# First stage of a fused two-layer block: scores of a head as one matmul of 48 stacked rows, filled by way of DRAM

## The chip, the cores and the metric

The kernel runs on one core of a Trainium2 chip. The core has a matrix engine (TensorE, PE in the profile; its weight loads are PEld), a vector engine (VectorE, DVE), a scalar engine (ScalarE, ACT), GpSimd (POOL) and a queue engine that only issues transfers (SyncE, SP). They run at the same time and wait for each other by semaphores. The metric is the device time of one execution in microseconds, the median of several runs.

## What is computed

The program is a block of two layers, each a gated attention with context tokens and a gated expert network. The change lies in the first attention. Cut to that:

```python
# x: 16 x 112 x 256, ctx: 16 x 375 x 256, 16 heads of 16
q = split_heads(layernorm(x) @ Wq.T + bq)          # 16 rows per head
k = split_heads(ctx @ Wk.T + bk)
v = split_heads(ctx @ Wv.T + bv)
scores = einsum('bhqd,bhkd->bhqk', q * 16**-0.5, k)
scores = scores + ((1 - mask) * -10000)[:, None]
attended = einsum('bhqk,bhkd->bhqd', softmax(scores), v)
x = x + tanh(g_xattn[0]) * merge_heads(attended)
# then: 2 of 8 linear experts per token; a second attention with 16 heads of 64; 2 of 8 two-layer experts
```

## The kernel before

Three stages follow one another: `phase_attention_small_heads` (first attention and the linear experts), `phase_attention_large_heads` (second attention and routing) and `phase_experts`. To keep float32 accuracy with float16 matmuls, each operand is split into a high part (HI) and the rest (LO), and a product is made of three: high by high, high by low, low by high (`PASSES`).

The first stage goes through 16 batches of 112 queries and 375 keys. Each engine runs its own program, written out by hand: `body(b, par)` for a batch, with sixteen slots `s`, one for each head. In slot `s` TensorE makes the scores of head `s` (`scores`, L593), transposes the probabilities of head `s - 2` (`transposes`, L602) and multiplies those of head `s - 4` with the values (`values`, L616). Between these it puts a piece of the projections of the next batch (`item`, L509: keys in slots 0 and 1, normalized x in 2, queries in 4, values in 5 to 7) and a piece of the experts of the batch before (`ditem`, slots 7 to 14). The order on TensorE is fixed. VectorE takes the scores from PSUM, adds the mask and finds the row maxima (`maxima`, L837), and makes the low part of the transposed probabilities (`plo`, L842). ACT makes the exponentials (L701) and the high part (`phi`, L708). There are two PSUM buffers for scores.

Scores of a head have 16 rows to contract. Before the change, one matmul contracts 128 rows. `k_stack` holds 64 rows of the keys' high part and below them 64 rows of their low part, for four heads at a time (a group `g`). The weights of the queries are doubled on the host, so that `q_f` (128 rows) has each group's 64 rows twice. `q_masked` holds for each head of a group these rows with those of the three other heads at zero; VectorE clears both of its buffers once at the start (L949). The first matmul takes the high part of the queries (against high and low keys), the second takes their low part. So a head needs two matmuls of 375 columns:

```python
for part in (HI, LO):
    last = pe.matmul(ps_s[h % 2][0:T, 0:C], q_masked[par][:, part, m, g * T:(g + 1) * T],
                     k_stack[par][:, g, :], start=(part == HI), stop=(part == LO))
```

`k_stack` and `q_masked` are filled from `k_s` and `q_s` by transfers between places in SBUF that SP issues: four for the keys (`stack_keys`, L344) and eight for the queries (`mask_queries`, L353) for each batch. SP's program for a batch is one list in a fixed order: mask, residual, tokens, context (`load_tokens`), keys, queries, a clearing of rows in DRAM for the third stage (`clear_rows`, L362, 1032 KB), store. The queries come from ACT (L665), which writes `q_f`, and GpSimd, which splits them (L431, L433). The transfers for batch `b + 1` are made during batch `b`; those for batch 0 stand ahead of the loop.

The second stage makes its scores (L1567) with 64 rows for each head, in pairs of heads on rows 0 to 63 and 64 to 127; all its other matmuls have over 64 rows. Its projections are at L1474, its values at L1582.

Of the kernel before, what the change touches and what calls it, by code (L numbers as in the profile page):

```python
# [112 lines left out]
def phase_attention_small_heads(nc, x, ctxT, mask, g_xattn, g_ffn, wq, wk, wv, bq, bk, bv, wg, we, be, consts,  # L113
                                x2_dram, next_w, next_w_dram, xs_dram):


    with ExitStack() as ctx:
# [8 lines left out]
        wqkv_f = sb("wqkv_f", [128, KT, 512 + 512 + E], F32)  # L126
        wqkv = sb("wqkv", [128, 2, KT, 512 + 512 + E], F16)
# [9 lines left out]
        wq_s = wqkv[:, :, :, 0:512].rearrange("p s k (g m) -> p s k g m", g=GROUPS)  # L137
        wk_s = wqkv[:, :, :, 512:768]
        wv_s = wqkv[:, :, :, 768:1024]
        wg_s = wqkv[:, :, :, 1024:1024 + E]  # L140
        bq_c = sb("bq_c", [128, GROUPS], F32)
# [18 lines left out]
        q_f = sb("q_f", [128, GROUPS * T], F32)  # L160
        q_s = sb("q_s", [128, 2, GROUPS * T], F16)
        q_masked = [sb(f"q_masked{i}", [128, 2, 4, GROUPS * T], F16) for i in range(2)]
        k_s = sb("k_s", [128, 2, 2, C], F16)
        k_stack = [sb(f"k_stack{i}", [128, GROUPS, C], F16) for i in range(2)]
# [60 lines left out]
        s_zq = sem("zq")  # L225
# [21 lines left out]
        s_qmask = sem("qmask")  # L247
        s_kstack = sem("kstack")
        s_score = sem("score")
# [29 lines left out]
        QMASK = 16 * 8  # L279
# [11 lines left out]
        WPARTS = ((512, 768), (0, 512), (768, 1024 + E))  # L291
# [13 lines left out]
        def _(sp):  # L305
            sp.dma_start(ctx_f[:, :, :], ctxT[0]).then_inc(s_cload, 16)
            sp.dma_start(wqkv_f[:, :, 512:768], wk).then_inc(s_wk, 16)
            sp.dma_start(x_in[:, :], x[0]).then_inc(s_xload, 16)
            sp.dma_start(wqkv_f[:, :, 0:512], wq).then_inc(s_wq, 16)
            sp.dma_start(wqkv_f[:, :, 768:1024], wv).then_inc(s_wv, 16)  # L310
            sp.dma_start(wqkv_f[:, :, 1024:1024 + E], wg).then_inc(s_wv, 16)
# [37 lines left out]

# [1984 lines left out]
```

## Time and profile before

| | |
|---|---|
| runs | 1442.60, 1450.26, 1454.12 us; median 1450.26 |
| profiled execution | 1443.42 us, of which the span from the first to the last instruction is 1441.8 us |
| mean granted TensorE clock | 0.944 of full speed |
| busy, share of the span | PE 88%, DVE 76%, ACT 70%, POOL 57% |
| DMA | 175.19 MB, mean 122 GB/s |

Busy time is the time in which an engine had at least one instruction under way. Matmuls overlap in the pipeline, so what one costs is the step from its start to the next one's start. The first stage ends at about 440 us, the second runs from about 500 to 1200 us, and the third takes the rest.

### The profile page before, as it was taken

To read this page: it belongs to the slowest core of one execution; us is meant where nothing else is said; L and a number is where in the kernel's file an instruction comes from. 1 tells how busy PE (TensorE), PEld (TensorE's weight loads), DVE (VectorE), ACT (ScalarE), POOL (GpSimd) and SP (SyncE) were. 2 spreads that over 40 slices of the span, in tenths; PEclk is the share of its full clock that TensorE was granted. 3 is DMA by queue.
4 is the path that set the end of the run, shared out by engine and by line. 5 is a ranking of instruction groups with operands and counts; after the bars stand their busy time and mean duration, and the time that the engine had idled before them with its cause. 6 is when DMAs were issued, how large, how long until landed. Compare 5 with 4: busy or idle time off the path is not lost. (4 is left out here: it accounts for less than half of the span.)

```text
span 1441.8 us, 44028 instructions
## 1 busy us (share of the span) xinstructions
PE 1264.8 (88%) x13508; PEld 916.7 (64%) x13508; DVE 1092.9 (76%) x3110; ACT 1003.9 (70%) x2584; POOL 827.7 (57%) x1204
## 2 busy tenths in 40 slices
PE   5999999999985599999998999999999985389994
PEld 3788888888864245656665556656566653278993
DVE  4899999999984268887887877878788873367772
ACT  3988788887883368787776777777787872155662
POOL 3645444454455445777676776777677675045663
PEclk9999999999997699999999999999999996599997
DMA  6233343333400148877666766767576784753323
GB/s 172 86 120 112 106 121 98 118 99 121 120 24 17 48 92 160 159 137 148 136 148 136 151 137 140 141 145 156 122 146 138 146 186 85 285 173 60 61 35 74
DMA packets 303968, 175.19 MB, mean 122 GB/s; under 512 B 250234, under 2 KB 291586, under 8 KB 300720
## 3 DMA queue, kind: packets, MB, share of 16 engines
q1 hardware_dynamic: 287632, 130.94, 40.8%
q0 software_dynamic: 13168, 35.80, 9.8%
q10 hardware_dynamic: 3024, 6.47, 1.6%
q8 instruction: 98, 1.61, 0.5%
q14 instruction: 46, 0.38, 0.1%
HBM read 64.48 MB, written 41.96 MB: 74 GB/s over the span
## 5 line engine op out<-in xcount | busy, mean ns | idle before, releaser
L1663 ACT ACTIVATE b_prob<-b_prob,b_top 112x487 f32<-112x487 f32 x256 | 178.9, 699 | 42.8 <-DVE b_top L1789 40.9
L1296 POOL TENSOR_TENSOR b_halves<-b_prob,b_halves 112x487 f16<-112x487 f32 x128 | 152.3, 1190 | 88.4 <-ACT b_halves L1688 86.6
L1474 PE MATMUL b_ps_p<-w_s,b_tok_s 128*128 128x512 f16 (+1 forms) x768 | 187.7, 381 | 5.6 <-DVE b_k_s L1776 5.3
L1474 PE MATMUL b_ps_p<-b_tok_s,w_s 128*128 128x487 f16 x768 | 188.0, 384 | 4.7 <-POOL b_tok_s L1290 3.7
L1789 DVE CUSTOM_DVE_ANT_0 b_prob<-b_ps_s,b_keep 112x487 f32<-112x487 f32 x256 | 167.7, 656 | 32.1 <-PE b_ps_s L1567 31.8
L701 ACT ACTIVATE a_prob<-a_prob,a_top 112x375 f32<-112x375 f32 x256 | 156.4, 611 | 4.5 <-DVE a_top L837 3.4
L1688 ACT ACTIVATE b_halves<-b_prob 112x487 f16<-112x487 f32 x256 | 156.0, 609 | 0.4
L837 DVE CUSTOM_DVE_ANT_0 a_prob<-a_ps_s,a_keep 112x375 f32<-112x375 f32 x256 | 138.6, 541 | 21.8 <-PE a_ps_s L593 19.2
L1582 PEld LDWEIGHTS b_ps_o<-b_v_s,b_pT 128*128 128x128 f16 (+1 forms) x3072 | 124.9, 100 | 32.7 <-DMA b_pT<-b_halves 11.0
L1582 PE MATMUL b_ps_o<-b_v_s,b_pT 128*128 128x64 f16 (+1 forms) x3072 | 136.1, 195 | 9.0 <-DMA b_pT<-b_halves 8.9
L842 DVE TENSOR_TENSOR a_pT<-a_ps_t,a_pT 125x336 f16<-125x336 f32 x256 | 128.6, 503 | 18.4 <-ACT a_pT L708 12.4
L602 PE MATMUL a_ps_t<-a_const,a_prob 112*125 112x112 f32 x768 | 127.8, 275 | 9.0 <-ACT a_prob L701 7.2
L602 PEld LDWEIGHTS a_ps_t<-a_const,a_prob 112*125 112x125 f32 x768 | 113.9, 189 | 31.3 <-ACT a_prob L701 22.5
L593 PE MATMUL a_ps_s<-a_k_stack,a_q_masked 128*112 128x375 f16 x512 | 126.5, 329 | 6.7 <-DMA a_q_masked<-a_q_s 6.1
L1474 PEld LDWEIGHTS b_ps_p<-b_tok_s,w_s 128*128 128x128 f16 x768 | 67.3, 100 | 96.4 <-issue 27.0
L1474 PEld LDWEIGHTS b_ps_p<-w_s,b_tok_s 128*128 128x128 f16 (+1 forms) x768 | 70.7, 105 | 85.1 <-DVE b_k_s L1776 14.1
L1776 DVE TENSOR_TENSOR b_k_s<-b_ps_p,b_k_s 128x487 f16<-128x487 f32 x128 | 84.5, 661 | 52.3 <-ACT b_k_s L1644 51.9
L1794 DVE TENSOR_TENSOR b_halves<-b_prob,b_halves 112x487 f16<-112x487 f32 x128 | 123.6, 965 | 0.0
L1567 PE MATMUL b_ps_s<-b_k_s,b_q_s 64*112 64x487 f16 x768 | 109.2, 391 | 14.8 <-issue 14.5
L708 ACT ACTIVATE a_pT<-a_ps_t 125x336 f16<-125x336 f32 x256 | 115.3, 450 | 9.8 <-PE a_ps_t L602 8.9
L1651 ACT ACTIVATE b_v_s<-b_ps_p 128x512 f16<-128x512 f32 (+1 forms) x128 | 76.2, 595 | 54.7 <-PE b_ps_p L1474 53.7
L1784 DVE TENSOR_TENSOR b_v_s<-b_ps_p,b_v_s 128x512 f16<-128x512 f32 (+1 forms) x128 | 87.9, 687 | 28.7 <-ACT b_v_s L1651 27.6
(262 smaller groups left out, 3063.0 us busy)
## 6 DMA issues: line engine op xcount, KB each, us to landing
xs<-a_blank SPq DMA_DIRECT2D x14, 1032.0 KB, 4.0
c_w_pool<-w_split SPq DMA_DIRECT2D x8, 1600.0 KB, 10.9
b_wch_f<-in_w_experts POOLq DMA_DIRECT2D x32, 384.0 KB, 4.9
w_split<-b_wch_s POOLq DMA_DIRECT2D x32, 384.0 KB, 4.0
a_ctx_f<-in_ctxT SPq DMA_DIRECT2D x16, 375.0 KB, 3.9
a_k_stack<-a_k_s SPq DMA_DIRECT2D x64, 93.8 KB, 2.8
b_ctx_t<-in_ctx SPq DMA_DIRECT2D x16, 375.0 KB
c_xt<-xs SPq DMA_DIRECT2D x35, 129.0 KB, 2.5
```

What stands on the lines that cost most here:

```text
L593: last = pe.matmul(ps_s[h % 2][0:T, 0:C], q_masked[par][:, part, m, g * T:(g + 1) * T], k_stack[par][:, g, :], start=(part == HI), stop=(p ...
L602: last = pe.transpose(ps_t[h % 2][0:KB0, j * T:(j + 1) * T], prob[:, h % RING, j * KB0:(j + 1) * KB0], ident[0:T, 0:T])
L701: act.activation(prob[:, h % RING, :], prob[:, h % RING, :], ACT.Exp, bias=top[:, h % RING:h % RING + 1], scale=-1.0, accum_out=sums[par][ ...
L837: dve.tensor_tensor_reduce(prob[:, h % RING, :], ps_s[h % 2][0:T, 0:C], keep[par][:, :], -SCALE0, 3e38, ALU.add, ALU.min, top[:, h % RING: ...
L842: dve.tensor_tensor(pT[0:KB0, h % RING, LO, :, 0:T], ps_t[h % 2][0:KB0, 0:NB0 * T].rearrange("p (j n) -> p j n", j=NB0), pT[0:KB0, h % RIN ...
L1296: pool.tensor_tensor(halves[:, h % TURN, LO, 0:NK], prob[:, h % RING, 0:NK], halves[:, h % TURN, HI, 0:NK], ALU.subtract).then_inc(s_lo[1], 1)
L1474: last = pe.matmul(out, sta(a, k), mov(m, k), start=(k == 0 and n == 0), stop=(k == tiles - 1 and n == 2))
L1582: last = pe.matmul(ps_o[h // 8][:, col:col + D1], pT[0:k, h % TURN, a, j, :], v_s[par][0:k, m, j, h * D1:(h + 1) * D1], start=(h % 8 == 0 ...
L1663: act.activation(prob[:, h % RING, 0:NK], prob[:, h % RING, 0:NK], ACT.Exp, bias=top[:, h % RING:h % RING + 1], scale=-1.0, accum_out=sums ...
L1688: act.activation(halves[:, h % TURN, HI, 0:NK], prob[:, h % RING, 0:NK], ACT.Copy).then_inc(s_hi, 1)
L1789: dve.tensor_tensor_reduce(prob[:, h % RING, 0:NK], ps_s[h % 3][0:T, 0:NK], keep[par][:, :], -SCALE1, 3e38, ALU.add, ALU.min, top[:, h % R ...
L1794: dve.tensor_tensor(halves[:, h % TURN, LO, 0:NK], prob[:, h % RING, 0:NK], halves[:, h % TURN, HI, 0:NK], ALU.subtract).then_inc(s_lo[0], 1)
```

## The change

A head's 16 rows of queries are stacked three times in 48 rows, as high, high, low, and its keys as high, low, high. One matmul over these 48 rows then makes all three products. Even heads lie in rows 0 to 47, odd heads in rows 64 to 111. The query weights are no longer doubled in SBUF: of each group only the first 64 columns are loaded, and the projection makes two blocks of 128 rows in place of four. Heads are spread over rows of `k_s` and `q_s`, so that the stacks are filled by way of two DRAM buffers, `keys` and `queries`: SP writes `k_s` or `q_s` out, waits until that has landed, and reads six pieces back (two halves, three parts).

```diff
+        q_stack = [sb(f"q_stack{i}", [128, H // 2, T], F16) for i in range(2)]
-        k_stack = [sb(f"k_stack{i}", [128, GROUPS, C], F16) for i in range(2)]
+        k_stack = [sb(f"k_stack{i}", [128, H // 2, C], F16) for i in range(2)]
...
+            def keys_out(c, par):
+                need_all(sp, settled, (s_ihi, 6, c, P_K + 2), (s_ifree, PI, c, P_K + 2), (s_kstack, NSTACK, c - 1, 0))
+                sp.dma_start(k_dram[par], k_s[:, :, :, :]).then_inc(s_kout, 16)
             def stack_keys(c, par):
-                need_all(sp, settled, (s_ihi, 6, c, P_K + 2), (s_ifree, PI, c, P_K + 2), (s_score, H, c - 1, 1))
+                need_all(sp, settled, (s_kout, 16, c, 16), (s_score, H, c - 1, 1))
+                rows = k_dram[par].rearrange("(r a d) s t c -> a s d r (t c)", a=2, d=D0)
                 for a in range(2):
-                    for part in (HI, LO):
-                        sp.dma_start(k_stack[par][64 * part:64 * part + 64, a::2, :],
-                                     k_s[64 * a:64 * a + 64, part, :, :]).then_inc(s_kstack, 16)
-            def mask_queries(c, par):
-                need_all(sp, settled, (s_qlo, 1, c, 1), (s_score, H, c - 1, 1))
-                for m in range(4):
-                    for row in (D0 * m, 64 + D0 * m):
-                        sp.dma_start(q_masked[par][row:row + D0, :, m, :], q_s[row:row + D0, :, :]).then_inc(s_qmask, 16)
+                    for i, part in enumerate(K_PARTS):
+                        sp.dma_start(k_stack[par][64 * a + D0 * i:64 * a + D0 * (i + 1), :, :].rearrange("d (r t) c -> d r (t c)", t=KT),
+                                     rows[a, part]).then_inc(s_kstack, 16)
+            # queries_out and stack_queries: the same with q_s, q_dram, q_stack, s_qout, s_qstack
...
             def body(b, par):
...
+                if ahead(b, 1):
+                    keys_out(b + 1, 1 - par)
                 if ahead(b, 2):
                     load_tokens(b + 2)
                 if ahead(b, 1):
                     stack_keys(b + 1, 1 - par)
-                    mask_queries(b + 1, 1 - par)
+                    queries_out(b + 1, 1 - par)
                 clear_rows(b)
+                if ahead(b, 1):
+                    stack_queries(b + 1, 1 - par)
...
-                    for g in range(GROUPS):
-                        last = product(ps[:, g * T:(g + 1) * T], lambda a, t: wq_s[:, a, t, g, :],
+                    for j in range(KT):
+                        last = product(ps[:, j * T:(j + 1) * T], lambda a, t: wq_s[:, a, t, j * 128:(j + 1) * 128],
                                        lambda a, t: xT[:, a, t, :])
...
-                for part in (HI, LO):
-                    last = pe.matmul(ps_s[h % 2][0:T, 0:C], q_masked[par][:, part, m, g * T:(g + 1) * T],
-                                     k_stack[par][:, g, :], start=(part == HI), stop=(part == LO))
-                last.then_inc(s_score, 1)
+                rows = slice(64 * (h % 2), 64 * (h % 2) + STACK)
+                pair = KT * (h % 8 // 2) + h // 8
+                pe.matmul(ps_s[h % 2][0:T, 0:C], q_stack[par][rows, pair, :], k_stack[par][rows, pair, :],
+                          start=True, stop=True).then_inc(s_score, 1)
...
-            for i in range(2):
-                dve.memset(q_masked[i][:, :, :, :], 0.0).then_inc(s_zq, 1)
...
+            for e in range(2):
+                rows = slice(64 * e, 64 * e + 64)
+                dve.tensor_copy(bq_c[rows, :], bq_g[rows, e::2]).then_inc(s_const, 1)
```

On TensorE, slot 4 and the start of slot 5 inside the batch loop before: the queries' projection (`a_xT`), the scores, transposes, values and the first piece of the next values' projection.

```order
L509 MATMUL a_ps_p<-a_xT,a_wqkv 128x112 x24
L593 MATMUL a_ps_s<-a_k_stack,a_q_masked 112x375 x2
L602 MATMUL a_ps_t<-a_const,a_prob 125x112 x3
L616 MATMUL a_ps_o<-a_v_s,a_pT 128x32 x12
L509 MATMUL a_ps_p<-a_wqkv,a_ctx_s 125x256 x6
```

The same place after the change:

```order
L534 MATMUL a_ps_p<-a_xT,a_wqkv 128x112 x12
L618 MATMUL a_ps_s<-a_k_stack,a_q_stack 112x375
L626 MATMUL a_ps_t<-a_const,a_prob 125x112 x3
L640 MATMUL a_ps_o<-a_v_s,a_pT 128x32 x12
L534 MATMUL a_ps_p<-a_wqkv,a_ctx_s 125x256 x6
```

Nothing changed places; the projection has half of its matmuls, and the scores have one in place of two, with transposes still right behind it.

On SP, the transfers of batch 1's `body` before, in the order of issue, with the semaphores that they wait for:

```order
L331 DMA a_keep<-in_mask 112x375 [waits a_keep,a_max]
L336 DMA a_x_res<-in_x 112x256
L324 DMA a_x_in<-in_x 112x256 [waits a_xn]
L326 DMA a_ctx_f<-in_ctxT 128x750 [waits a_csplit]
L344 DMA a_k_stack<-a_k_s 64x2x375 [waits a_score,a_ifree,a_ihi]
L344 DMA a_k_stack<-a_k_s 64x2x375 x3
L353 DMA a_q_masked<-a_q_s 16x2x448 [waits a_score,a_qlo]
L353 DMA a_q_masked<-a_q_s 16x2x448 x7
L362 DMA xs<-a_blank 128x2064
L357 DMA x<-a_x 112x256 [waits a_x2]
```

The same after the change:

```order
L340 DMA a_keep<-in_mask 112x375 [waits a_keep,a_max]
L345 DMA a_x_res<-in_x 112x256
L350 DMA keys<-a_k_s 128x1500 [waits a_kstack,a_ifree,a_ihi]
L333 DMA a_x_in<-in_x 112x256 [waits a_xn]
L335 DMA a_ctx_f<-in_ctxT 128x750 [waits a_csplit]
L358 DMA a_k_stack<-keys 16x4x750 [waits a_score,a_kout]
L358 DMA a_k_stack<-keys 16x4x750 x5
L364 DMA queries<-a_q_s 128x448 [waits a_qstack,a_qlo]
L382 DMA xs<-a_blank 128x2064
L372 DMA a_q_stack<-queries 16x4x224 [waits a_score,a_qout]
L372 DMA a_q_stack<-queries 16x4x224 x5
L377 DMA x<-a_x 112x256 [waits a_x2]
```

SP now has the write of the keys ahead of the token loads, waits for `a_kout` before the keys' pieces and for `a_qout` before those of the queries, and the clearing of `xs` stands between the write of the queries and their pieces. Ahead of the loop, for batch 0, the four steps follow one another with nothing between them.

## Rows read from the trace of the kernel before

**Rows 1.** Stretches: length; busy us PE, PEld, DVE, ACT, POOL; clock; DMA share; GB/s.

```profile
72.00:384.00 312.00, 307.95 (x3239) 256.18 (x3238) 290.34 (x1005) 257.25 (x799) 141.42 (x206) 1.00 0.36 112
205.97:231.65 25.68, 25.39 (x275) 21.13 (x270) 23.92 (x84) 21.26 (x67) 11.68 (x17) 1.00 0.32 100
205.97:213.94 7.97, 7.87 (x95) 6.25 (x91) 7.97 (x28) 7.30 (x23) 2.21 (x4) 1.00 0.40 112
217.04:220.17 3.13, 2.94 (x39) 2.78 (x37) 3.13 (x13) 3.02 (x11) 2.90 (x5) 1.00 0.00 0
```

**Rows 2.** Timeline of TensorE in slots 1 and 4: start us, duration us, instruction.

```profile
207.88 0.48 PE L593 MATMUL a_ps_s<-a_k_stack,a_q_masked 128*112 128x375 f16 x2
208.19 0.48 PE L602 MATMUL a_ps_t<-a_const,a_prob 112*125 112x112 f32 x3
208.51 0.31 PE L616 MATMUL a_ps_o<-a_v_s,a_pT 125*128 125x32 f16 x6
...
212.74 1.35 PE L509 MATMUL a_ps_p<-a_xT,a_wqkv 128*128 128x112 f16 x24
213.94 0.49 PE L593 MATMUL a_ps_s<-a_k_stack,a_q_masked 128*112 128x375 f16 x2
```

**Rows 3.** Timeline of TensorE in the second stage, in narrow windows (rows overlap).

```profile
702.14 0.52 PE L1582 MATMUL b_ps_o<-b_v_s,b_pT 128*128 128x64 f16 x12
...
702.47 0.19 PE L1582 MATMUL b_ps_o<-b_v_s,b_pT 103*128 103x64 f16 x1
702.59 0.41 PE L1567 MATMUL b_ps_s<-b_k_s,b_q_s 64*112 64x487 f16 x2
...
702.84 0.57 PE L1567 MATMUL b_ps_s<-b_k_s,b_q_s 64*112 64x487 f16 x4
...
703.04 0.37 PE L1567 MATMUL b_ps_s<-b_k_s,b_q_s 64*112 64x487 f16 x2
703.34 0.38 PE L1474 MATMUL b_ps_p<-b_tok_s,w_s 128*128 128x487 f16 x1
```

**Rows 4.** Timeline of TensorE in slot 2: two transposes of x after a wait.

```profile
210.58 0.32 PE L531 MATMUL a_ps_p<-a_const,a_xn 112*128 112x112 f32 x1
...
210.73 0.26 PE L531 MATMUL a_ps_p<-a_const,a_xn 112*128 112x112 f32 x1
210.82 0.32 PE L593 MATMUL a_ps_s<-a_k_stack,a_q_masked 128*112 128x375 f16 x1
```

**Rows 5.** One batch: SP's timeline, then transfers by size and us to landing.

```profile
212.02 2.75 SPq L344 DMA_DIRECT2D a_k_stack<-a_k_s  x4
219.88 5.15 SPq L353 DMA_DIRECT2D a_q_masked<-a_q_s  x8
...
xs<-a_blank SPq DMA_DIRECT2D x1, 1032.0 KB, 4.0
...
a_q_masked<-a_q_s SPq DMA_DIRECT2D x8, 28.0 KB, 2.0
...
x<-a_x SPq DMA_DIRECT2D x1, 112.0 KB, 1.9
```

**Rows 6.** Start-up, 8 to 30 us: timeline, then transfers by size and us to landing.

```profile
14.06 2.76 SPq L344 DMA_DIRECT2D a_k_stack<-a_k_s  x4
...
19.75 5.18 SPq L353 DMA_DIRECT2D a_q_masked<-a_q_s  x8
...
26.34 0.88 PE L593 MATMUL a_ps_s<-a_k_stack,a_q_masked 128*112 128x375 f16 x2 [6.12 <-DMA a_q_masked<-a_q_s]
...
a_next_f<-in_we ACTq DMA_DIRECT2D x1, 2048.0 KB, 9.5
a_ctx_f<-in_ctxT SPq DMA_DIRECT2D x1, 375.0 KB, 10.4
a_k_stack<-a_k_s SPq DMA_DIRECT2D x4, 93.8 KB, 7.6
```

**Rows 7.** Waits from 72 to 384 us: total us, times, longest us.

```profile
DVE a_prob L837 <- PE a_ps_s L593: 8.6, 24, 0.5
```

More of the change, by code:

```diff
@@ L136, in phase_attention_small_heads @@
         be_s = sb("be_s", [128, 2, D], F16)
[L137 to L141, printed above, removed]
+        wq_s = wqkv[:, :, :, 0:D]
+        wk_s = wqkv[:, :, :, D:2 * D]
+        wv_s = wqkv[:, :, :, 2 * D:3 * D]
+        wg_s = wqkv[:, :, :, 3 * D:3 * D + E]
+        bq_g = sb("bq_g", [128, GROUPS], F32)
+        bq_c = sb("bq_c", [128, KT], F32)
         bk_c = sb("bk_c", [128, KT], F32)
@@ L159, in phase_attention_small_heads @@
         xT = sb("xT", [128, 2, KT, T], F16)
-        q_f = sb("q_f", [128, GROUPS * T], F32)
-        q_s = sb("q_s", [128, 2, GROUPS * T], F16)
-        q_masked = [sb(f"q_masked{i}", [128, 2, 4, GROUPS * T], F16) for i in range(2)]
+        q_f = sb("q_f", [128, KT, T], F32)
+        q_s = sb("q_s", [128, 2, KT, T], F16)
+        STACK = 3 * D0
+        Q_PARTS, K_PARTS = (HI, HI, LO), (HI, LO, HI)
+        q_stack = [sb(f"q_stack{i}", [128, H // 2, T], F16) for i in range(2)]
         k_s = sb("k_s", [128, 2, 2, C], F16)
-        k_stack = [sb(f"k_stack{i}", [128, GROUPS, C], F16) for i in range(2)]
+        k_stack = [sb(f"k_stack{i}", [128, H // 2, C], F16) for i in range(2)]
         v_s = [sb(f"v_s{i}", [128, NB0, H, 2, D0], F16) for i in range(2)]
@@ L246, in phase_attention_small_heads @@
         s_qlo = sem("qlo")
-        s_qmask = sem("qmask")
+        s_qstack = sem("qstack")
         s_kstack = sem("kstack")
+        s_kout = sem("kout")
+        s_qout = sem("qout")
         s_score = sem("score")
@@ L278, in phase_attention_small_heads @@
         NSETUP = 16 * 4
-        QMASK = 16 * 8
+        NSTACK = 16 * 6
         DI = 8
@@ L382, in _ @@
             load_tokens(1)
+            keys_out(0, 0)
             stack_keys(0, 0)
-            sp.wait_ge(s_zq, 2)
-            mask_queries(0, 0)
+            queries_out(0, 0)
+            stack_queries(0, 0)
             sp.wait_ge(s_blank, 1)
@@ L663, in item @@
                     need(act, s_qlo, 1, c, 0)
-                    for g in range(GROUPS):
-                        last = act.activation(q_f[:, g * T:(g + 1) * T], ps[:, g * T:(g + 1) * T], ACT.Identity, bias=bq_c[:, g:g + 1])
+                    for j in range(KT):
+                        last = act.activation(q_f[:, j, :], ps[:, j * T:(j + 1) * T], ACT.Identity, bias=bq_c[:, j:j + 1])
                     last.then_inc(s_ifree, 1)
@@ L672, in item @@
                     if j == 0:
-                        need(act, s_kstack, 64, c, 0)
+                        need(act, s_kout, 16, c, 0)
                     act.activation(k_s[:, HI, j, :], ps[:, 0:C], ACT.Identity, bias=bk_c[:, j:j + 1]).then_inc(s_ihi, 1)
@@ L2261, in build_program @@
     acc = nc.dram_tensor("acc", (NTOK + SLOTS, D), F32, kind="Internal").ap()
+    keys = nc.dram_tensor("keys", (2, 128, 2, KT, C), F16, kind="Internal").ap()
+    queries = nc.dram_tensor("queries", (2, 128, 2, KT, T), F16, kind="Internal").ap()
     xs = nc.dram_tensor("xs", (DUMMY + SLOTS, ROW), F32, kind="Internal").ap()
@@ L2276, in build_program @@
                                         a["wv0"], a["bq0"], a["bk0"], a["bv0"], a["wg0"], a["we0"], a["be0"], a["consts"],
-                                        x2, w1_s, a["w1"], xs)
+                                        x2, w1_s, a["w1"], xs, keys, queries)
             phase_attention_large_heads(nc, a["ctx"], a["mask1"], a["g_xattn"], a["g_ffn"], a["g1"], a["b1"], a["g2"],
```

47 lines of the change are left out of this document (29 added, 18 removed).

## The prediction

> **What bounds the kernel now.** The changed code works only in the first stage, which fills the time from 0 to about 440 us of the 1441.8 us span. I first read busy time by stretch. From 72 to 384 us, with the batches in a steady rhythm, TensorE is busy 307.95 of 312 us and VectorE 290.34, at a granted clock of 1.00 [rows 1]. So TensorE sets the pace, but VectorE is close behind, and busy shares can't tell what a cheaper or dearer product is worth. One batch does: batch b's scores begin at 205.97 and the next batch's at 231.65, a period of 25.68 us with VectorE busy 23.92 us [rows 1]. A batch has sixteen slots, one for each head. In slots 0 to 4 (205.97 to 213.94) and 7 to 8 (217.04 to 220.17) VectorE is busy all of the 7.97 and 3.13 us [rows 1]. In those seven slots TensorE is not alone in setting the pace. In the other nine it is.
>
> The timeline of TensorE shows what a slot is made of. Scores take 0.31 us from their first start to that of the transposes: two matmuls of 375 columns, 0.155 us each, the transposes 0.32 us [rows 2]. The queries' projection, 24 matmuls of 112 columns, takes 1.20 us, 0.05 each [rows 2]. Starts are what I count; the durations of matmuls overlap.
>
> **What the change removes.** One of the two score matmuls of each head: 16 x 0.155 = 2.5 us of TensorE for each batch. Twelve of the 24 query matmuls: 12 x 0.05 = 0.6 us for each batch. Half of the work of ACT and GpSimd on queries goes too; both are off the path and I cost it at nothing. The two clears of q_masked ran in the first 5 us, where VectorE was waiting for weights: nothing. The query weights come in two transfers in place of one, and VectorE makes two small copies of the query bias before it reads the first keys: at most 0.3 us once, inside the uncertainty of the start-up below.
>
> **What it adds on TensorE.** Every matmul of the first stage's steady part so far uses the array's 128 rows. The built program gives the new 48-row product a tile of 64 rows, as it gives the 64-row products of the second stage (L1567). Those show what it costs to change between the two kinds, and that is the row on which this prediction rests. At 702 us twelve values matmuls start 0.03 us apart (twelve in 0.52 us, of which the last one lasts 0.19); the last starts at 702.47, and the first 64-row product only at 702.59: 0.12, thus **0.09 us to enter**. The 64-row products go in pairs, the two halves of the array at once: pairs start at 702.59, 702.84 and 703.04. The last step, 0.20 us, is 487 columns; the first is 0.25, so **0.05 us for weights** that could not be loaded ahead. The next 128-row matmul starts at 703.34, which is 0.30 after the last pair: **0.09 to 0.10 us to leave** [rows 3]. One place stands here for the many pairs of heads of the second stage. After the new scores come transposes with fp32 weights. What those cost when nothing was loaded ahead shows at 210.58: the first starts 0.15 us before the second, the second 0.09 before the next one, so **0.05 to 0.06** more [rows 4].
>
> Rule and row on the two loads of weights: the trace shows 0.05 us for a load of 112 or 128 columns that is not hidden [rows 3, 4]. The Trainium skill, "TensorE: Matmul & The Clock Gate", section "LDWEIGHTS (loading the stationary operand)", gives columns divided by 1.2 GHz, which is an estimate of 0.09 and 0.10 us. By the rows the two loads add 0.10 us to a head, by the page 0.19, which would put fifteen batches of sixteen heads 22 us later. I go by the rows.
>
> So a head's scores cost 0.09 + 0.05 + 0.16 + 0.09 + 0.05 = 0.44 us where they cost 0.31 to 0.32. The removed matmul gives 0.16 back and the two changes of tile take 0.28: **TensorE loses 0.12 us for each head**, 1.9 us for each batch, and 1.9 - 0.6 = 1.3 us with the queries' saving. The lower bound for the unknown single 48-row product is that it enters and leaves for nothing; that is the first rival.
>
> **What of it reaches the end.** If TensorE alone set the pace, all 1.3 us would. In the seven slots in which VectorE is full, TensorE's extra 0.12 us falls into waits that it has now. So does the saving on the queries, which sits in slot 4. Nine slots x 0.12 = 1.05 us is then left; if the saving on queries still counts in full, it is 0.45. I take 0.9 us for each batch, the middle between the ends 0.45 and 1.3. Of the 16 batches I count 15, since the first has no feed-forward items: **+13.5 us, ends 7 and 19.**
>
> **The way through DRAM, steady part.** SP issues everything in order. Before, a batch has four key transfers from 212.02 (2.75 us, 0.67 to 0.69 each), eight query transfers from 219.88 (5.15 us, 0.64 each), which land 2.0 us after their issue, so at about 227; the scores that need them start at 231.65 [rows 1, 5]. After: keys to DRAM at 212.0, landing after 1.9 us (112 KB) to 4.0 us (1032 KB) [rows 5], say by 215.5; six key transfers until 219.6; queries to DRAM and the 1032 KB clearing of rows at 219.9; the queries are there at 222.0; six transfers of 0.64 until 225.9, landing at about 228. That is 3.5 us ahead of need, a little more in a longer batch. Cost nothing, as long as this slack holds. Queued behind the two new waits on SP are load_tokens (needed a batch later), the clearing (needed in the third stage) and store; none is near its time.
>
> **The way through DRAM, start-up.** Here nothing hides it. TensorE's first scores at 26.34 waited 6.12 us for the masked queries [rows 6]. Before, keys are issued at 14.06 to 16.8 and queries at 19.75 to 24.93, and the scores start 1.4 us after the last issue ended. From 11 us on 2048 KB of expert weights are loading: between 8 and 30 us transfers of 94 KB land after 7.6 us, and of 375 KB after 10.4 [rows 6]. The keys to DRAM (375 KB) go into that at 14.1. With the 7.6 they are there at about 21.7; six transfers until 25.8; queries to DRAM, 1.9 us, 27.8; six more, 3.9 us, 31.7; and 1.4 to the scores: 33.1. That is **+7 us**. Ends: with the 1.9 us of the steady part [rows 5] for the keys it is +1; with 10.4 it is +9.5. All of it counts, since every slot stands behind these scores on TensorE.
>
> Sum against the profiled execution: 1443.4 + 13.5 + 7 = 1464 us, ends 1451 and 1472. That execution is at the low end of the runs shown (1442.6 to 1454.1, median 1450.3), so against the median I add the same 20.5: **1471 us**, ends 1458 and 1479. About 1% (14.5 us) is what a measurement of this kernel can tell from no change.
>
> **Rivals.** *No cost of changing tiles* (it does what it says): the entry and the exit were seen only with pairs on both halves, and a lone product on one half may behave otherwise. Then TensorE has 3.1 us less for each batch. VectorE is full in seven slots, so only nine x 0.16 = 1.4 us can go, which also keeps the period above VectorE's 23.92: -21 us, with start-up -14, 1436 us. For it: no row shows such a lone product. Against it: the built program uses the same tile size, and the time to leave is after the last product, when both halves have ended. The Trainium skill, "TensorEngine Tiling (Array Packing)", section "Key Properties", says that a change of tiling mode drains the engine; by that this rival would be out, and it gives no size. Chance 0.10.
>
> *TensorE's waits swallow it*: the period has room, since TensorE's parts are shorter than the slots wherever VectorE is full. If the extra 0.12 only replaces waits elsewhere too, the steady part gives 0 to 3 us and start-up stays: 1458 us. Against it: between 72 and 384 us VectorE waited for the scores 24 times, 8.6 us in all [rows 7]; in those slots TensorE is late already, and the extra time can't fall into a wait of its own. Chance 0.18.
>
> *Queries late in every batch*: SP's two round trips take over 3.5 us more than I reckon, as transfers did at start-up (7.6 us [rows 6] against 2.0 [rows 5]). Every us beyond costs 15: with 2 us over, +30 and so about 1500. For it: SP is now in one chain from the keys to the last query transfer. Against it: the DMA engines are busy 0.36 of the steady part [rows 1]. Chance 0.06.
>
> *Dearer weight loads*: if each of the two loads that nothing hides cost a whole step of the transposes, 0.09 [rows 4], in place of 0.05, a head costs 0.08 more, a batch 1.3 us, fifteen 19 us: 1490. For it: the load of the 112 columns of a lone product is in no row. Against it: both places that show a load in the open give 0.05 [rows 3, 4]. Chance 0.05. This is the case of the page named above.
>
> **How the numbers follow.** My forecast, tiles changed twice for each head and partly absorbed, has 0.61. Its own ends are 1458 and 1479, and a tenth to a fifth of it lies below the 1% line at 1464.8. Within 1%: that part, most of the absorbed case and half of the no-cost case, 0.32. Faster by over 1%: the other part of the no-cost case, 0.05. Slower: 0.63. The range, 1450 to 1483, leaves out the no-cost rival and the two dear ones.
>
> **What the changed profile would show.** Scores matmul: one record each head, from it to the transposes about 0.30 us (0.05 + 0.16 + 0.09), the transposes' first step 0.15 in place of 0.10; from the matmul before to the scores 0.09 more. First scores near 33 us, waiting for queries from DRAM. Period near 26.6. VectorE's busy time unchanged and its waits for the scores' matmul longer. No wait of the scores for a DMA after the first batch. The granted clock stays at 1.00 from 72 to 384 us; if the emptier array lets it fall to 1.2 GHz in places, the loss is larger than all this. Wrong it is if from scores to transposes I find 0.16 us.

## The result, and the profile after

The changed kernel takes **1470.93 us** (median of 4 runs, 1465.86 to 1480.85), the kernel before 1446.72 beside it. The ratio is 1.017, with a 95% interval of 1.0098 to 1.0242. The profiled execution took 1470.93 us, 27.5 more than that of before (1443.42). The prediction was 1471.

The first stage carries most of the loss. Its timeline of TensorE at the first scores of batches 0, 2, 14 and 15, and at the first scores of the second stage, in the changed kernel (start us, duration us, instruction):

```profile
31.65 0.56 PE L618 MATMUL a_ps_s<-a_k_stack,a_q_stack 48*112 48x375 f16 x1 [14.72 <-DMA a_q_stack<-queries]
...
85.17 0.36 PE L618 MATMUL a_ps_s<-a_k_stack,a_q_stack 48*112 48x375 f16 x1
...
407.41 0.36 PE L618 MATMUL a_ps_s<-a_k_stack,a_q_stack 48*112 48x375 f16 x1
...
434.78 0.36 PE L618 MATMUL a_ps_s<-a_k_stack,a_q_stack 48*112 48x375 f16 x1
...
541.01 0.41 PE L1592 MATMUL b_ps_s<-b_k_s,b_q_s 64*112 64x487 f16 x2
```

The same four places of the kernel before; batch 0 is in [rows 6]:

```profile
77.00 0.35 PE L593 MATMUL a_ps_s<-a_k_stack,a_q_masked 128*112 128x375 f16 x1
...
386.07 0.35 PE L593 MATMUL a_ps_s<-a_k_stack,a_q_masked 128*112 128x375 f16 x1
...
413.26 0.35 PE L593 MATMUL a_ps_s<-a_k_stack,a_q_masked 128*112 128x375 f16 x1
...
517.82 0.41 PE L1567 MATMUL b_ps_s<-b_k_s,b_q_s 64*112 64x487 f16 x2
```

Start these differences at the top. The first scores come 5.3 us later (31.65 against 26.34). Twelve periods last 322.24 us in place of 309.07: 26.85 each in place of 25.76, **+1.10 for each batch**, and all fifteen steps from batch 0 to 15 last 403.13 in place of 386.92, which is +16.2. So the last batch begins 21.5 us later, the second stage 23.2. The other 4.3 us came behind that, in stages whose code is the same. Their length varies by more than that: from its first scores to the first matmul of the third stage, the second stage lasts between 711.7 us (e5_late_load) and 725.2 us (e7_after_twice) in the profiles of this document, 712.0 in the kernel before and 715.5 in the changed one.

What a slot is made of, on the timeline of TensorE after, which answers to [rows 2]:

```profile
202.07 0.36 PE L618 MATMUL a_ps_s<-a_k_stack,a_q_stack 48*112 48x375 f16 x1
202.37 0.58 PE L626 MATMUL a_ps_t<-a_const,a_prob 112*125 112x112 f32 x3
202.78 0.31 PE L640 MATMUL a_ps_o<-a_v_s,a_pT 125*128 125x32 f16 x6
```

From the scores to the transposes are 0.30 us, although there is one product now where there were two (0.31), and the three transposes last 0.41 in place of 0.32. Between the matmul before and the scores 0.08 to 0.09 more is lost: where six values matmuls stand there, their first start is 0.24 us ahead of the scores in place of 0.15. In all a head costs TensorE about 0.16 us more (0.15 to 0.17 by what stands around it).

The records of the weight loads (PEld) show where the transposes lose their time. This one starts with the first transpose, and not before it:

```profile
202.37 0.40 PEld L626 LDWEIGHTS a_ps_t<-a_const,a_prob 112*125 112x125 f32 x3 [0.17 <-issue]
```

From 72 to 384 us the part of TensorE that loads weights stood idle before such a load 163 times without a wait that the profile shows ("issue"), 27.9 us in all, where the kernel before has one such case of 0.2 us:

```profile
PEld a_ps_t L626 <- issue: 27.9, 163, 0.2
```

The stretch from 72 to 384 us and the wait for the scores after, which answer to [rows 1] and [rows 7]:

```profile
72.00:384.00 312.00, 311.37 (x2782) 214.53 (x2781) 279.22 (x966) 244.95 (x741) 128.04 (x196) 1.00 0.45 128
```

```profile
DVE a_prob L861 <- PE a_ps_s L618: 15.5, 35, 0.6
```

TensorE is busy 311.37 of 312 us, with fewer matmuls (2782 against 3239). VectorE waits for scores 15.5 us in place of 8.6. The clock stays at 1.00. SP's list after, for one batch in the steady part, which answers to [rows 5]:

```profile
198.18 0.35 SPq L350 DMA_DIRECT2D keys<-a_k_s  x1
...
201.20 2.68 SPq L358 DMA_DIRECT2D a_k_stack<-keys  x6
205.90 0.34 SPq L364 DMA_DIRECT2D queries<-a_q_s  x1
206.43 0.36 SPq L382 DMA_DIRECT2D xs<-a_blank  x1
207.62 3.43 SPq L372 DMA_DIRECT2D a_q_stack<-queries  x6
```

The last piece of the queries is issued by 211.05. The next batch's first scores come at about 219.4 (five periods of 26.85 after 85.17), so the way through DRAM has some 6 us to spare after a landing of 2 us. At the start it has nothing. SP's timeline there, and the transfers by size and us to landing, which answer to [rows 6]:

```profile
13.86 0.35 SPq L350 DMA_DIRECT2D keys<-a_k_s  x1
21.52 2.68 SPq L358 DMA_DIRECT2D a_k_stack<-keys  x6
24.24 0.42 SPq L364 DMA_DIRECT2D queries<-a_q_s  x1
27.51 2.65 SPq L372 DMA_DIRECT2D a_q_stack<-queries  x6
...
a_next_f<-in_we ACTq DMA_DIRECT2D x1, 2048.0 KB, 9.6
...
keys<-a_k_s SPq DMA_DIRECT2D x1, 375.0 KB, 7.6
```

The keys are written out at 13.86, and SP can issue nothing else until they have landed, 7.6 us later.

### The profile page after: what moved, and what is told of

It is laid out like the page before. It is cut to its first block and busy times, and to the rows that moved or that the text cites. A ratio compares the mean times of both kernels' runs of the same rounds, so it can differ in the third digit from the quotient of the medians.

```text
span 1469.3 us, 43167 instructions
## 1 busy us (share of the span) xinstructions
PE 1285.8 (88%) x13060; PEld 876.6 (60%) x13060; DVE 1091.4 (74%) x3110; ACT 1000.8 (68%) x2552; POOL 818.3 (56%) x1204
## 5 line engine op out<-in xcount | busy, mean ns | idle before, releaser
L626 PE MATMUL a_ps_t<-a_const,a_prob 112*125 112x112 f32 x768 | 153.3, 310 | 3.8 <-ACT a_prob L725 3.1
L626 PEld LDWEIGHTS a_ps_t<-a_const,a_prob 112*125 112x125 f32 x768 | 106.7, 193 | 50.8 <-issue 36.0
L1809 DVE TENSOR_TENSOR b_v_s<-b_ps_p,b_v_s 128x512 f16<-128x512 f32 (+1 forms) x128 | 87.9, 687 | 28.6 <-ACT b_v_s L1676 27.5
L618 PE MATMUL a_ps_s<-a_k_stack,a_q_stack 48*112 48x375 f16 x256 | 95.8, 374 | 14.7 <-DMA a_q_stack<-queries 14.7
```

The lines of the kernel that those rows point to most:

```text
L626: last = pe.transpose(ps_t[h % 2][0:KB0, j * T:(j + 1) * T], prob[:, h % RING, j * KB0:(j + 1) * KB0], ident[0:T, 0:T])
```

## The experiments

Two explanations stood against each other for the steady part: the change of the array's tile (twice for each head), or something that comes with the stacking itself (DRAM traffic, SP's longer list). The period, not the total, is what tells them apart, since it varies by only some hundredths of a us between runs: it is 26.85 in the first profile of the changed kernel and in those of e4, e5, e8 and e9, which do the same work in the steady part.

**e1_full_tile.** The scores contract rows 0 to 111, so they use the whole array like every other matmul of the stage. The other half of `q_stack` is zero, cleared once.

```diff
-                rows = slice(64 * (h % 2), 64 * (h % 2) + STACK)
-                pe.matmul(ps_s[h % 2][0:T, 0:C], q_stack[par][rows, pair, :], k_stack[par][rows, pair, :],
+                pe.matmul(ps_s[h % 2][0:T, 0:C], q_stack[par][0:64 + STACK, h % 2, pair, :], k_stack[par][0:64 + STACK, pair, :],
...
+            for i in range(2):
+                dve.memset(k_stack[i][:, :, :], 0.0).then_inc(s_zq, 1)
+                dve.memset(q_stack[i][:, :, :, :], 0.0).then_inc(s_zq, 1)
```

> Everything of the change stays (48 stacked rows, the way through DRAM, queries not doubled), but the scores' matmul contracts rows 0 to 111 of the stacks, so it has the array's full tile: a buffer of queries for even and one for odd heads, whose other rows are zero since the start. Theory 1 (the two changes of tile for each head cost the time): no gap of 0.08 us before the scores, 0.16 us from scores to transposes in place of 0.29, the transposes' first step 0.10 in place of 0.20; TensorE gets 0.31 us for each head back, VectorE becomes the bound, the period falls from 26.85 us to 24.2 to 24.8; first scores still near 31.6 us; time about 1471 - 15 x 2.3 = 1436, between 1430 and 1445. Theory 2 (the traffic through DRAM and its waits cost it): period and time stay, 1465 to 1475.

Measured: 1451.42 us (10 runs, 1444.27 to 1458.22), ratio to before 1.0025 (0.9994 to 1.0056), so no difference from the kernel before is shown. A slot in its timeline of TensorE:

```profile
203.15 0.33 PE L619 MATMUL a_ps_s<-a_k_stack,a_q_stack 112*112 112x375 f16 x1
203.32 0.47 PE L627 MATMUL a_ps_t<-a_const,a_prob 112*125 112x112 f32 x3
203.63 0.31 PE L641 MATMUL a_ps_o<-a_v_s,a_pT 125*128 125x32 f16 x6
```

From scores to transposes are 0.17 us (0.30 in the changed kernel), the transposes last 0.31 (0.41), and the step into the scores is back to what it was before the change. The load for the first transpose now starts together with the scores' matmul, 0.16 us ahead of the transposes:

```profile
203.16 0.19 PEld L627 LDWEIGHTS a_ps_t<-a_const,a_prob 112*125 112x125 f32 x1
```

That is 0.33 us for each head, all of it the price of the tile: the data, the traffic and SP's list are the same. The period is 25.22, below the 25.76 of before, so the tile is what made the steady part slower. The size was missed, though: 16 x 0.33 = 5.2 us of TensorE went from a batch, and the period fell by 1.64 where 2.1 to 2.7 was expected. From 72 to 384 us the kernel has VectorE at 292.69 of 312 and TensorE at 287.98:

```profile
72.00:384.00 312.00, 287.98 (x2967) 230.59 (x2967) 292.69 (x1034) 258.83 (x791) 137.45 (x210) 1.00 0.47 138
```

TensorE is no longer busier than VectorE, and it has new waits: in this stretch its weight loads for the transposes waited 30 times for ScalarE's exponentials, 12.1 us in all, where the changed kernel has 22 such waits with 4.5 us in all. What exactly holds the period at 25.2 was not tried. The first scores came at 33.46, 7.1 us later than in the kernel before; in this kernel VectorE clears buffers ahead of its first work. The shorter batches pay for that, and the second stage starts at 518.08, 0.3 us later than before.

**e2_full_twice.** The same, with each head's product made twice, so that TensorE has about the score work of the kernel before, and everything else is stacked.

```diff
+                for n in range(2):
+                    last = pe.matmul(ps_s[h % 2][0:T, 0:C], q_stack[par][0:64 + STACK, h % 2, pair, :], k_stack[par][0:64 + STACK, pair, :],
+                                     start=True, stop=True)
+                last.then_inc(s_score, 1)
```

> As the full-tile kernel, but each head's product is made twice (the second overwrites the first), so that the scores cost TensorE the two matmuls that they cost before the change. What is left of the change is the way through DRAM and half of the queries' projection. Theory 1 (changes of tile): scores to transposes 0.32 us, period 25.2 to 25.8, time that of before plus the later start, less some of the 0.6 us of the queries for each batch: 1443 to 1453. Theory 2 (traffic through DRAM): period 26.8, time 1465 to 1475.

Measured: 1461.13 us (10 runs), ratio 1.008 (1.0048 to 1.0113), period 25.68. This is the sharpest comparison with the kernel before (25.76). The difference is the DRAM traffic, SP's list and half of the work on the queries, and together they are -0.08 us a batch. The slots tell them apart. Taken from the starts of the scores, as means over ten batches, slots 0 to 3, 6 and 9 to 15 last the same in both kernels, within 0.03 us. Slot 4, with the queries' projection, is 0.59 us shorter; slot 5 is 0.38 longer and slots 7 and 8 are 0.07 longer each. So the traffic costs nothing that can be seen in the steady part, and of the 0.6 us of query matmuls saved all but about 0.1 is lost again within four slots. The time is 8 us above the 1443 to 1453 that theory 1 gave. 7.7 us of the 12.2 above before were there when the second stage began (525.5), since the first scores came at 33.90, 7.6 us late; the rest lies in the stages behind.

**e7_after_twice.** The changed kernel, its 48-row product made twice.

```diff
+                for n in range(2):
+                    last = pe.matmul(ps_s[h % 2][0:T, 0:C], q_stack[par][rows, pair, :], k_stack[par][rows, pair, :],
+                                     start=True, stop=True)
+                last.then_inc(s_score, 1)
```

> The changed kernel with every head's scores made twice in the 64-row tile (the second product overwrites the first), nothing else: 16 more products of 0.16 a batch. Theory A (in the changed kernel TensorE's chain sets the period in nearly every slot: the period is constant at 26.85 and few slots wait for VectorE): the period grows by nearly all of what is added, 16 x 0.16 = 2.6, to 29.1 to 29.5, while the same second product in the full-row kernel (e2 against e1) cost only 0.47 of it. Theory B (VectorE's full slots absorb a part here as they do there): 27.3 to 28.2, and more than the 35 of 162 slots wait. Time by A: 1471 + 15 x 2.5 = 1508; by B: 1480 to 1491.

Measured: 1516.74 us (one run), period 28.90. The added 2.6 us of TensorE gave +2.05, under what theory A asked and over theory B's. So 8 tenths of it reach the period here, and only 0.46 of about 2.5 us, 2 tenths, in the full tile. Side by side the periods read: full tile 25.22; with 16 x 0.16 more 25.68; changed kernel 26.85; with 16 x 0.16 more 28.90. The same added work costs more the fuller TensorE already is. Slot by slot, the added 0.16 us arrives in full in thirteen of the sixteen slots here. In the full tile it arrives in eight, and slots 2, 4, 7, 12 and 15 get 0.13 to 0.20 us shorter. In this last kernel TensorE is busy all 312 us, VectorE 265:

```profile
72.00:384.00 312.00, 312.00 (x2761) 208.20 (x2760) 264.93 (x896) 231.71 (x688) 120.98 (x185) 1.00 0.41 119
```

**e3_values_first.** In the changed kernel the values stand between the scores and the transposes, to give the fp32 weights of the transposes six matmuls to be loaded behind.

```diff
-                    if not (first(b) and s < 2):
-                        c, _, h = heads(s, 2, b, par)
-                        transposes(c, h)
...
                     if s != 4 and not (first(b) and s < 4):
                         values(*heads(s, 4, b, par))
+                    if not (first(b) and s < 2):
+                        c, _, h = heads(s, 2, b, par)
+                        transposes(c, h)
```

> The changed kernel with one edit: in each slot the values' matmuls (float16 weights of 128 columns) stand between scores and transposes. Theory 1a (leaving the 64-row tile costs about 0.08 us plus a load of weights in the open, and the transposes' fp32 weights make that load dear): scores to values 0.29 us, first step of the values 0.03 to 0.04, first step of the transposes back from 0.20 to 0.10; 1.3 to 1.6 us less TensorE work for each batch, period 25.6 to 26.4, time 1450 to 1463. Rival 1b (the 0.10 us belongs to leaving the tile whatever follows): it turns up on the values, period 26.85, time 1468 to 1475. ACT gets the transposes 0.16 us later, which could cost some of it.

Measured: 1471.68 us (4 runs), ratio 1.0158 (1.0095 to 1.022), period 26.96: nothing gained. Its timeline:

```profile
202.36 0.36 PE L618 MATMUL a_ps_s<-a_k_stack,a_q_stack 48*112 48x375 f16 x1
202.66 0.32 PE L640 MATMUL a_ps_o<-a_v_s,a_pT 125*128 125x32 f16 x6
202.82 0.56 PE L626 MATMUL a_ps_t<-a_const,a_prob 112*125 112x112 f32 x3
203.22 0.82 PE L534 MATMUL a_ps_p<-a_wqkv,a_ctx_s 128*125 128x256 f16 x6
```

From the scores to the values are again 0.30 us, so leaving the 64-row tile costs the same whatever comes next. The six values take 0.16 as always (their weights cost 0.01 in the open), and the transposes still last 0.40. So their weights aren't hidden behind six matmuls of 0.025 us either. Their load starts with the last of the six, 0.02 us ahead of the transposes:

```profile
202.80 0.29 PEld L626 LDWEIGHTS a_ps_t<-a_const,a_prob 112*125 112x125 f32 x2
```

Neither expectation holds as it stood: the time and the period are those of rival 1b, but the 0.10 us did not turn up on the values. It stayed with the transposes. Where one whole-array scores matmul (0.16 us) stands right ahead of them, in the kernel before and in e1, the load is hidden.

**e5_late_load.** The start-up: the 2048 KB load of expert weights is issued later, when ScalarE comes to the queries.

```diff
-            act.dma_start(we_f[:, :, :], we).then_inc(s_wload, 16)
             for k in range(PI):
                 item(0, 0, k)
+                if k == P_Q:
+                    act.dma_start(we_f[:, :, :], we).then_inc(s_wload, 16)
```

> The changed kernel with one edit: ACT issues the 2048 KB load of expert weights after it has written the first queries (near 17 us) in place of 11 us. Theory (at start-up the write of the keys to DRAM is slow since it shares the DMA engines with that load): the keys land 3 to 4 us after their issue in place of 7.6, first scores near 27.5 in place of 31.65, and 4 us less in all. Rival (the write itself or its place in the queue is slow): still 7 to 8 us, first scores at 31.6.

Measured: 1475.76 us (one run), first scores 32.33, so the forecast of 27.5 missed. Its transfers from 8 to 36 us:

```profile
a_next_f<-in_we ACTq DMA_DIRECT2D x1, 2048.0 KB, 11.6
...
keys<-a_k_s SPq DMA_DIRECT2D x1, 375.0 KB, 2.7
...
queries<-a_q_s SPq DMA_DIRECT2D x1, 112.0 KB, 9.0
```

The keys now land in 2.7 us in place of 7.6, and the queries in 9.0 in place of 3.2. The wait moved to whichever write lay beside the load. So a large part of the price of the start-up is sharing with that load, and the load must come behind both round trips. The Trainium skill, "DMA: Bandwidth & Descriptors", section "Issuing engines are not separate DMA queues", says that transfers of all engines end on the same 16 DMA engines and interleave; the trace agrees, since the load was issued by ScalarE and the slowed writes by SP.

**e4_start.** Here SP issues the load, behind the last stack piece, and the queries go out ahead of the keys' pieces.

```diff
             keys_out(0, 0)
-            stack_keys(0, 0)
             queries_out(0, 0)
+            stack_keys(0, 0)
             stack_queries(0, 0)
+            sp.dma_start(we_f[:, :, :], we).then_inc(s_wload, 16)
...
-            act.dma_start(we_f[:, :, :], we).then_inc(s_wload, 16)
```

> The changed kernel, 48-row tiles and all, with two edits to its start-up only: the issuing order is keys out, queries out, then the two sets of stack pieces, and the 2048 KB weight load is issued by SyncE behind the last of the stack pieces in place of ahead of everything on ScalarE. Theory A (the start-up's loss is contention and queue order, not the stacking itself): with nothing beside it the 375 KB of keys lands in the 2.7 us that the run with the later load showed, so at about 16.5 us; the queries, issued right behind, at 17 to 18, the stack pieces at about 20 to 22; the first scores start at 24 to 26 us in place of 31.65, about 1 us ahead of the kernel before (26.34). The load lands some 6 us later than before, but its first reader comes inside batch 0, so batch 0 may be longer by up to 3 us. The period stays 26.85. Time: 1471 - 4 to 7 = 1464 to 1467. Theory B (the round trip by way of DRAM costs its own latency whatever lies beside it): first scores at 30 us or later, time 1470 to 1473. If the load's first reader waits for what was saved, batch 0 grows by as much as the first scores come earlier, and the time also stays at 1471; the trace tells the two apart by the first scores and the length of batch 0.

Measured: 1470.78 us (4 runs), ratio 1.0151 (1.009 to 1.0211). SP's start-up and the first scores:

```profile
13.75 0.35 SPq L350 DMA_DIRECT2D keys<-a_k_s  x1
17.17 0.32 SPq L364 DMA_DIRECT2D queries<-a_q_s  x1
17.53 2.79 SPq L358 DMA_DIRECT2D a_k_stack<-keys  x6
20.37 2.78 SPq L372 DMA_DIRECT2D a_q_stack<-queries  x6
23.19 0.43 SPq L411 DMA_DIRECT2D a_next_f<-in_we  x1
```

```profile
24.91 0.56 PE L619 MATMUL a_ps_s<-a_k_stack,a_q_stack 48*112 48x375 f16 x1 [5.68 <-DMA a_q_stack<-queries]
```

The first scores come 6.7 us earlier, 1.4 before those of the kernel before, so the two ways through DRAM need not make the start longer. How much of it comes from the later load and how much from the new order was not tried. The late load costs batch 0 almost nothing: it lasts 25.48 us against 25.35 in the changed kernel, and the second stage starts at 535.15, 5.9 us earlier. So theory A holds for the trace. But the median (1470.78) is that of the changed kernel (1470.93), and so both kernels were run again, on the same chip.

**e8_after_again** and **e9_start_again.** The changed kernel and e4_start again, neither edited.

> The changed kernel unaltered, beside the next one on the same chip: 1467 to 1474, period 26.85, first scores 31.65. The later stages run with the clock granted below 1 and their length differs from run to run (stage 2's period 44.16 to 45.0 in the kernels so far with the same code), so 5 rounds are needed for a difference of 6.

> The kernel of e4_start unaltered. Theory A (the 6.7 us that the first scores came earlier are a saving, and e4's 1470.8 was spread): 5 to 7 us under e8_after_again, 1463 to 1467. Theory B (it is given back in the later stages, whose clock is granted by what went before): within 2 us of e8_after_again with the first scores again at 24.9 and the second stage again starting 5.8 earlier; the second and third stage then take 4 to 6 us longer.

Measured: 1476.39 us (1467.63 to 1483.63, ratio 1.019, interval 1.0151 to 1.0229) and 1471.47 us (1463.95 to 1479.09, ratio 1.0157, interval 1.0123 to 1.0191). The first scores and the first of the second and third stage, in the changed kernel and then in that with the new start:

```profile
31.52 0.56 PE L618 MATMUL a_ps_s<-a_k_stack,a_q_stack 48*112 48x375 f16 x1 [12.18 <-DMA a_q_stack<-queries]
...
548.89 0.41 PE L1592 MATMUL b_ps_s<-b_k_s,b_q_s 64*112 64x487 f16 x2
...
1267.43 0.17 PE L2134 MATMUL c_ps_a<-cum,ones 112*128 112x8 f16 x1 [7.13 <-PEq L1022]
```

```profile
24.23 0.56 PE L619 MATMUL a_ps_s<-a_k_stack,a_q_stack 48*112 48x375 f16 x1 [6.09 <-DMA a_q_stack<-queries]
...
542.64 0.41 PE L1592 MATMUL b_ps_s<-b_k_s,b_q_s 64*112 64x487 f16 x2
...
1264.93 0.17 PE L2134 MATMUL c_ps_a<-cum,ones 112*128 112x8 f16 x1 [7.15 <-PEq L1022]
```

7.3 us ahead at the first scores, 6.25 at the second stage, 2.5 at the third. The second stage took 718.5 us in one profile and 722.3 in the other, with the same code. The medians differ by 4.9, near theory A's 5 to 7, but the intervals overlap. The changed kernel is above the 1467 to 1474 that was expected of it; the last section shows what its batch 0 lost. So the saving is shown up to the second stage, and likely but not shown in the total. Whether the later stages really give a part back, or only spread, is open.

**e6_full_start.** Both cures together: the full tile of e1, the start of e4, and the clearing of the second pair of buffers behind VectorE's items of batch 0.

> The full-row tile of the run e1_full_tile (scores contract rows 0 to 111, the other half of the queries' stack zeroed, so that no matmul of the stage leaves the whole-array tile) together with the start-up edits of e4_start, and the clearing of the second pair of buffers moved behind VectorE's items of batch 0. Theory A (two separate causes, each worth its own amount): first scores at 25 to 27 us in place of e1's 33.46, which is 6 to 8 us; the period stays e1's 25.2 against 25.76 before, 15 x 0.55 = 8 us ahead of the kernel before. Time: 1451.4 - 6 to 8 = 1443 to 1446, which is a ratio of 0.995 to 0.998 to the kernel before at 1449: the stacking is worth having only with both costs removed, and then by less than 1%. Theory B (part of e1's time above the kernel before is in later stages or start-up that can't be moved): time 1449 to 1452, no difference from the kernel before. If the zeroed halves slow the start-up on VectorE (the clearing lay ahead of the weights' low halves), the first scores come no earlier than 30 us.

Measured: **1439.06 us** (12 runs, 1432.44 to 1445.61), ratio to before **0.9942** (0.9913 to 0.9971). The interval lies below 1: this kernel is 0.6% faster than the kernel before, a little more than theory A asked (1443 to 1446). The changed kernel stood at a ratio of 1.017. The first scores come at 23.79, the last batch at 403.43 and the second stage at 509.59, 8.2 us ahead of before:

```profile
23.79 0.56 PE L621 MATMUL a_ps_s<-a_k_stack,a_q_stack 112*112 112x375 f16 x1 [7.27 <-DMA a_q_stack<-queries]
...
403.43 0.35 PE L621 MATMUL a_ps_s<-a_k_stack,a_q_stack 112*112 112x375 f16 x1
...
509.59 0.41 PE L1600 MATMUL b_ps_s<-b_k_s,b_q_s 64*112 64x487 f16 x2
```

Its period is 25.21, that of e1. 2.6 us come from the start (26.34 to 23.79) and 7.3 from fifteen shorter batches (379.64 against 386.92), 9.8 together at the last batch; the median, against 1447.46 for before, gives 8.4. The 7.3 us are what stacking with the full tile is worth. The 2.6 us can't be put down to it: in the kernel before, the same 2048 KB load runs beside the transfers of keys too (7.6 us to landing [rows 6]), and that kernel with a later load was not run.

## Why the prediction was right

The direction and the cause were right, and the size was near. That 1471 and 1470.93 agree so closely is luck: the start-up was put 1.7 us too high and the fifteen batches 2.7 us too low, 2.7 us of the difference of the medians come from no term, and the kernel before measured 3.5 us less than the median to which the sum was added. Two steps of the working were wrong, the load in front of the transposes and the slots that absorb the extra time.

- **The tile costs more than the removed matmul saves.** Right, and e1 shows it by itself. To enter was put at 0.09 and measured 0.08 to 0.09. From the scores to the transposes was put at 0.30 and measured 0.30.
- **The load in front of the transposes** was the one term of the sum that was too small: 0.05 by [rows 4], and 0.09 to 0.10 in the profile after. A head loses 0.16 in place of 0.12. The load of [rows 4] was not like the one it stood for: it has 128 columns, and that of the transposes has 125. That fits the difference, though no run changed the columns alone. In the trace of the kernel before, the records of fp32 loads last 0.14 us at 128 columns and 0.19 at 125 (lowest, median and highest in ns; from 72 to 384 us):

```profile
L531 PEld LDWEIGHTS a_ps_p<-a_const,a_xn x24: 137/140/143, 81.6 to 365.1; 112*128 112x128 f32 x24
...
L602 PEld LDWEIGHTS a_ps_t<-a_const,a_prob x579: 183/188/190, 73.1 to 382.4; 112*125 112x125 f32 x193
```

The rule weighed in the prediction is half right. The Trainium skill, "TensorE: Matmul & The Clock Gate", section "LDWEIGHTS (loading the stationary operand)", gives columns divided by 1.2 GHz, an estimate of 0.10 us for these 125 columns, and here the trace agrees. For the scores' own 112 fp16 columns the estimate is 0.09. Second products in e7 start 0.20 after the first ones (0.16 of it is columns), so about 0.04 us of the load is not hidden, and for the step between matmuls the measurement decides against the estimate.

- **A part is absorbed where VectorE is full.** That a part is absorbed is right: 16 x 0.16 - 0.6 = 2.0 us of TensorE gave +1.10, and e2 and e7 show the share that gets through growing from 2 tenths to 8. Where it is absorbed was wrong. Slot by slot (starts of the scores, means over ten batches), the changed kernel differs from the kernel before by:

| slots | change of each slot, us | together |
|---|---|---|
| 1, 3, 6, 7, 9, 10, 11, 13, 14 | +0.14 to +0.17 | +1.47 |
| 0, 2, 8, 12, 15 | -0.03 to +0.07 | +0.03 |
| 4 and 5 | -0.78 and +0.37 | -0.41 |

The extra time does come in nine slots, as counted, but three of them (1, 3, 7) are slots in which VectorE is full, and 12 and 15, where it should have come, got nothing. So VectorE's busy share did not tell which slots absorb, and that the count came out is luck. With 0.16 for a head, nine slots give 1.47; the queries' saving takes 0.4 of it back. The value of 0.9 was the middle of a range, and came out 0.2 low.

- **The queries' saving.** The lower end (0.45 us a batch) counted all 0.6 us of it. e2 speaks against that end: all that is left of the 0.6 at the end of the batch is about 0.1.
- **The way through DRAM, steady part: nothing.** Right by e2. The pieces were even issued faster than reckoned: six in 2.68 us for the keys and 3.43 for the queries, where 4.1 and 3.9 stood.
- **Start-up +7.** Measured +5.3. The 7.6 us for the keys was right to a tenth. It came from transfers of 94 KB beside the same load, and was used for one of 375 KB, so the tenth is luck. The pieces took 2.7 us a set where 3.9 to 4.1 stood, the queries 3.2 where 1.9 stood.
- **Sum.** +20.5 stood against +21.5 at the last batch's first scores and +27.5 in the profiled pair. The last 6 us lie behind the first stage's last batch and come from no term of mine. In medians it is +24.2.
- **Rivals.** No tile cost: out by the trace. Waits swallow it: out, since the fifteen steps from batch 0 to 15 grew by 16.2 us where this rival has 0 to 3; VectorE's wait for scores grew from 8.6 to 15.5. Queries late: out, no scores after the first batch waited for a transfer. Dearer loads: true of the transposes' load alone, and a part of that was absorbed.

## What to carry to other kernels

A lone 64-row product between whole-array matmuls costs about 0.33 us more here than the same product padded with zeros to the full height, twice what the product itself takes (0.16). 0.10 us of that is the fp32 load behind it; with fp16 weights of 128 columns behind it (e3) that part is 0.01, though the fp32 load then stays in the open further on. If stacking makes operands short, pad them, and only then count what was saved. Before a cost is borrowed from another row, compare the shapes, down to the columns of the weights. Where two engines are nearly full, take the share of a saving that reaches the period from a kernel with a known amount of work added, not from busy time. A transfer in a chain that nothing hides belongs ahead of bulk loads.

## What the runs showed of the hardware

The fp32 weights of a transpose (125 columns) cost 0.09 to 0.10 us in the open, and six matmuls of 0.025 us don't hide them. The fp16 weights of the values (128 columns) cost 0.01 in the same place. In the trace of the kernel before, the records of weight loads of 128 columns are the short ones in both types: fp16 0.10 us against 0.13 at 112 and 0.14 at 125 columns, fp32 0.14 against 0.19 at 125.

TensorE's granted clock is at half (1.2 GHz) for some time in the first two batches of the stacked kernels, in other places and for other lengths in each run. In the first profile of the changed kernel it is 0.50 from 20 to 36 us, most of which TensorE spends waiting for transfers, 1.00 from 40 to 48, and 0.50 again from 52 to 60. Before it fell, TensorE was busy 3.56 of the 4 us from 44 to 48. In the kernel before it is 0.50 from 24 to 28 and 1.00 from 32 to 60. In the profiles of e8_after_again and e9_start_again scores, transposes and values have the same mean durations from 34 to 60 us (559, 460 and 194 ns), and batch 0 takes 31.88 us in both where the first profile of the changed kernel has 25.35. But the recorded clock differs. The stretch in e8, then in e9:

```profile
34.00:60.00 26.00, 26.00 (x142) 18.37 (x142) 14.68 (x43) 18.36 (x50) 9.99 (x12) 1.00 0.36 109
```

```profile
34.00:60.00 26.00, 26.00 (x161) 18.66 (x159) 13.97 (x42) 18.72 (x51) 13.62 (x15) 0.50 0.34 98
```

The 559 ns of the scores stand against 363 at full clock. So a 1.00 in the clock column is not proof of a full clock. The duration of a matmul of known size is. This is worth up to 6.5 us of a total, on top of the spread of the second stage (711.7 to 725.2 us with the same code), and it is why differences under 6 us are read from the timeline here and not from totals.
